# Gating's token mix made in the experts' stage, and one convolution tile on TensorE: a three-stage fp32 kernel

## The chip, the cores and the metric

One core of one Trainium2 chip. The metric is device microseconds of one execution, lower is better. The engines are TensorE (PE; its weight loads PEld), VectorE (DVE), ScalarE (ACT), GpSimd (POOL) and SyncE (SP), which here issues most DMAs. L12 is line 12 of the kernel; a "q" behind an engine is its sequencer.

## The reference

Four residual blocks follow one another on x of 16 sequences (B), 512 steps (T), 512 features (D), in fp32, with `cond` of 16 x 512.

```python
# 1: state space block; the 16 taps of the convolution are the cond rows, per feature
conv = conv_b + sum(x_pad[:, k:k + L, :] * conv_w[k, 0] for k in range(16))
proj = conv @ Wp + bp;  B_t = softplus(proj[..., :64]);  C_t = tanh(proj[..., 64:])
u = x @ Ws + bs
state = decay * state + dt * b_t * u_t          # scan over steps, y = C_t * state
x = x + y @ Wo + bo
# 2: LSTM with 512 units, step by step
x = x + lstm(x, cond, Wx, Wh, b)
# 3: token shift, hashed experts (16, 512 tokens each), gate
xprev = concatenate([cond[:, None, :], x[:, :-1]], axis=1)
xk = x + (xprev - x) * time_maa_k
xr = x + (xprev - x) * time_maa_r
y = scattered_back(square(relu(expert_in @ w_key[e])) @ w_value[e])   # expert_in: rows of xk
x = x + sigmoid(xr @ w_recept.T) * y
# 4: per sequence and feature, over time: softmax of |x|, a chosen place, a mask
x = x + x * (abs(x) >= abs(x) at the place where cumsum(softmax) passes cond)
```

## The kernel before, in words

Features lie on partitions, in KD = 4 blocks of 128. Three stages run one after the other; each is a block of per-engine instruction lists written by hand, with semaphores between the engines, and a stage begins on every engine only when all engines have ended the one before.

**Recurrence** (`recur_phase`). Time is cut into 32 tiles of 16 steps; a tile's 16 steps of all 16 sequences are 256 columns. Block 1 of tile n+2 or n+3 is worked out beside the LSTM steps of tile n. `convolve(m, q, first, last)` is 64 VectorE operations per tile on 128x256 (L595 the first tap, L599 the others), half q = 0, 1 covering two feature blocks. `project(m, q)` (L337) multiplies the result by Wp, `inputs(m, q)` (L345) the window by Ws, `outputs(m, q)` (L357, L358) the state by Wo, `input_products(m, par, q)` (L841 to L843) x1 by Wx, as three products of split halves, q = 0 to 15. ScalarE has `soft_first` (L464 to L468), `soft_last` (L472), `state_high`, `split_high` (L485) and `keep_inputs` (L491, one per input product); VectorE the five parts of `state_part` (from L605), `add_block` (L652), `split_low` (L666) and `split_wx` (L776).

Ahead of the first tile the work of tiles 0, 1 and part of 2 is done in an order of its own. VectorE: convolve(0), two split_wx, state(0), two split_wx, add_block(0), split_low(0), convolve(1), convolve(2, 0), state(1), add_block(1), split_low(1), convolve(2, 1), and then the first step's transpose (L683). TensorE: project(0) and inputs(0) by halves, outputs(0), inputs(1), all 16 input products, project(1), outputs(1), inputs(2), project(2, 0), then the first half of a step (L387). ScalarE issues the loads of Wx and Wh at its beginning. GpSimd waits for Wh and then stores 16 MB of zeros to the experts' rows in memory (L305). SP loads windows (L210) and centers (L203).

The block-2 result x2 goes from `stream` to memory, tile by tile, in 64-byte pieces (L236, the last L248); xk rows go to the experts' buffer by indirect DMA (L298).

**Experts** (`expert_phase`). For each of 16 experts: 512 rows are turned (L926), 8 groups of products with wk, relu and square on ScalarE (L980, L984), 4 groups of products with wv, copied by ScalarE (L994) and stored by GpSimd (L913). Weights are split into halves by ScalarE (L968, L985) and VectorE. SP loads wk (L899) for expert e once wk of e-1 is split, rows (L892), and wv (L904).

**Finish** (`finish_phase`). For each sequence i: SP loads x2; ScalarE scales the shifted x2 (`weigh_last`, L1184), VectorE makes xr from it (`mix_in`, L1250); `receptance(i)` multiplies it by wr on TensorE (L1147, four groups of 128x512 in fp32), two banks in turn, each freed by ScalarE's `open_gate` (L1192). GpSimd gathers the experts' rows (L1107), TensorE turns them (L1158), VectorE's `combine(i)` (L1261, L1264) makes x3. Then block 4: `absolute` (ScalarE, L1199), `invert` (L1268, L1272), `exponent` (L1207), `scan` (L1279), `take_sides` (ScalarE, L1216), `choose`, `search` (L1294), `keep` (L1303), and the product on GpSimd (L1133). The main loop on VectorE is, for each i, scan(i), bound(i), combine(i+1), mix_in(i+3), choose(i), invert(i+1), search(i), keep(i); on ScalarE

```python
            for i in range(B):
                if i + 2 < B:
                    open_gate(i + 2, 0, 2)
                take_sides(i)
                if i + 1 < B:
                    absolute(i + 1)
                if i + 2 < B:
                    open_gate(i + 2, 2, KD)
                if i + 1 < B:
                    exponent(i + 1)
                if i + 4 < B:
                    weigh_last(i + 4)
```

and on TensorE turn(i+2), receptance(i+3).

Of the kernel before, what the change touches and what calls it, by code (L numbers as in the profile page):

```python
# [20 lines left out]
F32 = mybir.dt.float32  # L21
# [54 lines left out]
def build(nc, ins, out):  # L76

    x2_d = nc.dram_tensor("x2_scratch", (P, KD, B, T), F32, kind="Internal").ap()
# [3 lines left out]
    with ExitStack() as ctx:  # L82
# [10 lines left out]
        expert_phase(nc, ctx, ins, carve, banks, keep, rows_d, y_d)  # L93
        carve.top = base
        finish_phase(nc, ctx, ins, carve, banks, keep, x2_d, y_d, out)


def recur_phase(nc, ctx, ins, carve, banks, keep, x2_d, slot_d, rows_d, y_d):
# [5 lines left out]
    wh = carve(KD, 4 * H)  # L104
    wx_lo = carve(KD, 4 * H, dt=F32R)
# [37 lines left out]
    expert_no, slot_base, onehot, segment, count = (carve(E, SEG, at=at + 2048 + 4096 * i) for i in range(5))  # L143

    gate_ps, xw_ps = banks[0:2], banks[2:4]
    proj_ps, u_ps = banks[4][:, 0:LTILE], banks[5][0:N_STATE, 0:LTILE]
# [14 lines left out]
             "rows_turned", "rows_ready", "index_ready", "scattered", "pool_passed", "sp_passed", "center_landed"]  # L161
    s = {n: ctx.enter_context(nc.semaphore("rc_" + n)) for n in names}
    halves = ["window_landed", "x2_stored", "g_done", "turned", "pre_ready", "ifo_ready", "g_ready", "terms_ready",
# [3 lines left out]
    x_dram = ins["xT"]  # L167
# [21 lines left out]

    def two(q):  # L190
        return slice(2 * q, 2 * q + 2)
# [4 lines left out]
    with nc.Block() as block:  # L196
        @block.sync
        def _(sp):
# [6 lines left out]
            def load_window(m, q):  # L205
                sp.wait_ge(s["conv_done"], CONVS * (m - 1) + CONVS // 2 * (q + 1))
                sp.sem_inc(s["sp_passed"], 1)
                sp.wait_ge(s["u_part"], 2 * (m - 1) + q + 1)
# [5 lines left out]
            for q in range(2):  # L214
                sp.dma_start(window[:, two(q), HALO:], x_dram[:, two(q), 0:LTILE]).then_inc(s["window_landed"][q], 16)
            load_center(0)
            for m in range(1, 4):
                for q in range(2):
                    load_window(m, q)
                if m < 3:  # L220
                    load_center(m)
# [10 lines left out]
            def tile(n, pair, four, ahead):  # L232
                if later(n, 1):
                    sp.wait_ge(s["x2_done"], 2 * n)
                    sp.sem_inc(s["sp_passed"], 1)
                    sp.dma_start(x2_d.rearrange("p c b t -> p (c b) t")[:, :, bass.ds((n - 1) * LSTEPS, LSTEPS)],  # L236
                                 stream[four - 1].rearrange("p c b t -> p (c b) t")[:, :, 1:])\
                        .then_inc(s["x2_stored"][(four + 1) % 2], 16)
# [9 lines left out]
            sp.dma_start(x2_d.rearrange("p c b t -> p (c b) t")[:, :, (NLT - 1) * LSTEPS:],  # L248
# [79 lines left out]
        def _(pe):  # L328
# [70 lines left out]
            for q in range(2):  # L399
                project(0, q)  # L400
                inputs(0, q)
# [991 lines left out]
```

## Time and profile before

| | |
|---|---|
| median of 3 runs | 4121.78 us (4120.27 to 4122.02) |
| the profiled execution's own time | 4119.96 us |
| its span, first to last instruction | 4118.3 us |
| mean granted TensorE clock | 0.98 of full speed |
| busy: PE, DVE, ACT, POOL | 94%, 74%, 41%, 7% |
| first step of the recurrence (DVE) | 118.98 us |
| first load of the experts' stage | 3011.67 us |
| first load of the finish | 3783.95 us |
| first and last round's scan in the finish | 3825.25, 4096.19 us |

All stage times are from the profiled execution, counted from its span's start. The profiled execution is 1.8 us shorter than the median of the runs. The three stages do not overlap, so what shortens one shortens the whole.

### The profile page before, as it was taken

To read this page: it belongs to the slowest core of one execution; us is meant where nothing else is said; L and a number is where in the kernel's file an instruction comes from. 1 tells how busy PE (TensorE), PEld (TensorE's weight loads), DVE (VectorE), ACT (ScalarE), POOL (GpSimd) and SP (SyncE) were. 2 spreads that over 40 slices of the span, in tenths; PEclk is the share of its full clock that TensorE was granted. 3 is DMA by queue.
4 is the path that set the end of the run, shared out by engine and by line. 5 is a ranking of instruction groups with operands and counts; after the bars stand their busy time and mean duration, and the time that the engine had idled before them with its cause. 6 is when DMAs were issued, how large, how long until landed. Compare 5 with 4: busy or idle time off the path is not lost. (4 is left out here: it accounts for less than half of the span.)

```text
span 4118.3 us, 111735 instructions
## 1 busy us (share of the span) xinstructions
PE 3858.1 (94%) x44034; PEld 2530.6 (61%) x44034; DVE 3047.6 (74%) x9953; ACT 1677.9 (41%) x5296; POOL 292.5 (7%) x362
## 2 busy tenths in 40 slices
PE   3999999999999999999999999999769999997995
PEld 3566666666656666665666666666457888875442
DVE  9888888888878888887888888875545544552798
ACT  3334433333433333333333333433234434443675
POOL 1000000000000000000000000000000000001343
PEclk8999999999999999999999999999989999998998
DMA  7121111112111111211111112100043343333353
GB/s 287 28 37 27 27 35 27 31 31 37 27 28 27 35 27 32 38 29 28 27 35 27 32 30 37 27 17 15 12 166 123 130 157 141 122 112 123 123 184 112
DMA packets 387862, 266.94 MB, mean 65 GB/s; under 512 B 288953, under 2 KB 322233, under 8 KB 384292
## 3 DMA queue, kind: packets, MB, share of 16 engines
q1 hardware_dynamic: 365648, 184.21, 17.8%
q0 software_dynamic: 17696, 66.79, 4.2%
q10 hardware_dynamic: 4020, 9.10, 0.6%
q8 instruction: 338, 5.54, 0.6%
q14 instruction: 160, 1.31, 0.1%
HBM read 176.48 MB, written 83.92 MB: 63 GB/s over the span
## 5 line engine op out<-in xcount | busy, mean ns | idle before, releaser
L387 PE MATMUL bank<-buf,buf 128*16 128x256 f32 x32768 | 1872.3, 380 | 62.5 <-DVE buf L705 52.9
L387 PEld LDWEIGHTS bank<-buf,buf 128*16 128x16 f32 x32768 | 906.0, 97 | 883.1 <-DVE buf L705 78.9
L841 PE MATMUL bank<-buf,buf 128*128 128x256 f32 (+1 forms) x3072 | 1036.7, 337 | 2.7 <-DVE buf L1012 2.7
L842 PE MATMUL bank<-buf,buf 128*128 128x256 f32 (+1 forms) x3072 | 978.3, 318 | 0.0
L843 PE MATMUL bank<-buf,buf 128*128 128x256 f32 (+1 forms) x3072 | 977.4, 318 | 0.0
L599 DVE SCALAR_TENSOR_TENSOR buf<-buf,buf,buf 128x256 f32<-128x256 f32 x1920 | 870.6, 480 | 0.8 <-issue 0.8
L683 DVE STREAM_TRANSPOSE buf<-bank 128x256 f32<-128x256 f32 x1024 | 459.9, 449 | 449.4 <-PE bank L387 409.3
L556 ACT ACTIVATE buf<-buf 128x96 f32<-128x96 f32 x1024 | 290.4, 284 | 1136.6 <-DVE buf L688 1136.0
L841 PEld LDWEIGHTS bank<-buf,buf 128*128 128x128 f32 x3072 | 581.2, 189 | 253.3 <-issue 215.2
L843 PEld LDWEIGHTS bank<-buf,buf 128*128 128x128 f32 x3072 | 583.3, 190 | 41.3
L842 PEld LDWEIGHTS bank<-buf,buf 128*128 128x128 f32 x3072 | 584.2, 190 | 38.5
L559 ACT ACTIVATE buf<-buf 128x32 f32<-128x32 f32 x1024 | 235.1, 230 | 631.7 <-DVE buf L700 631.7
L1024 DVE CAST buf<-buf 128x512 fp32r<-128x512 f32 x128 | 54.6, 427 | 355.8 <-ACT buf L984 352.3
L688 DVE SCALAR_TENSOR_TENSOR buf<-buf,buf 128x128 f32<-128x128 f32 x1024 | 295.3, 288 | 20.1
L1147 PE MATMUL bank<-buf,buf 128*128 128x512 f32 x512 | 231.6, 607 | 46.6 <-DVE buf L1250 23.8
L298 POOL DMA_INDIRECT expert_in_scratch<-buf,buf x64 | 81.1, 1268 | 2413.1 <-ACT buf L512 2370.2
L491 ACT ACTIVATE buf<-bank,buf 128x256 f32<-128x256 f32 x512 | 234.6, 458 | 19.0 <-PE bank L843 18.6
L705 DVE SCALAR_TENSOR_TENSOR buf<-buf,buf 128x32 f32<-128x32 f32 x1024 | 193.9, 189 | 61.8 <-ACT buf L559 14.2
L700 DVE SCALAR_TENSOR_TENSOR buf<-buf,buf 128x32 f32<-128x32 f32 x1024 | 196.5, 192 | 36.0 <-DVE buf L697 0.7
L557 ACT ACTIVATE buf<-buf 128x32 f32<-128x32 f32 x1024 | 218.3, 213 | 0.0
L1147 PEld LDWEIGHTS bank<-buf,buf 128*128 128x128 f32 x512 | 97.1, 194 | 169.8 <-issue 136.2
L694 DVE SCALAR_TENSOR_TENSOR buf<-buf,buf 128x32 f32<-128x32 f32 x1024 | 176.2, 172 | 18.1 <-ACT buf L556 15.0
(139 smaller groups left out, 2906.5 us busy)
## 6 DMA issues: line engine op xcount, KB each, us to landing
buf<-in_wk SPq DMA_DIRECT2D x16, 2048.0 KB, 9.6
buf<-in_wv SPq DMA_DIRECT2D x16, 2048.0 KB, 9.3
buf<-in_xT SPq DMA_DIRECT2D x62, 496.0 KB, 3.8
buf<-in_xB SPq DMA_DIRECT2D x32, 512.0 KB, 3.6
expert_in_scratch<-buf POOLq DMA_DIRECT2D x16, 1024.0 KB, 22.6
x_scratch<-buf SPq DMA_DIRECT2D x32, 512.0 KB, 9.6
buf<-expert_in_scratch SPq DMA_DIRECT2D x16, 1024.0 KB, 11.6
expert_out_scratch<-buf POOLq DMA_DIRECT2D x64, 256.0 KB, 4.7
```

What stands on the lines that cost most here:

```text
L387: last = mm(gate_ps[hf][32 * j:32 * j + B, 0:HCOLS], hist[:, k, at_step(slot_at)], wh[:, k, j * GCOLS + hf * HCOLS:j * GCOLS + (hf + 1) * ...
L491: a(xw[par][:, :, q, :], xw_ps[q % 2][:, 0:LTILE].rearrange("p (b t) -> p t b", b=B), ACT.Identity, bias=bias[:, q:q + 1], scale=0.5).then ...
L556: a(gate[hf], pre[hf][:, 0:6, :], ACT.Tanh, scale=0.5).then_inc(s["ifo_ready"][hf], 1)
L557: a(gcand[hf], pre[hf][:, 6:8, :], ACT.Tanh).then_inc(s["g_ready"][hf], 1)
L559: a(tanh_c[hf], cell[hf], ACT.Tanh, scale=0.5).then_inc(s["tc_ready"][hf], 1)
L599: v.scalar_tensor_tensor(out=conv[:, k, :], in0=src, scalar=taps[:, k, i:i + 1], in1=conv[:, k, :], op0=ALU.mult, op1=ALU.add).then_inc(s[ ...
L683: v.transpose(turned_g[hf].rearrange("p g b -> p (g b)"), gate_ps[hf][:, 0:HCOLS])\
L688: v.scalar_tensor_tensor(out=pre[hf], in0=turned_g[hf][:, :, 0:B], scalar=0.5, in1=xw[par][:, st, 8 * hf:8 * hf + 8, :], op0=ALU.mult, op1 ...
L841: nc.tensor.matmul(out, left[0], right[0], start=first, stop=False)
L842: nc.tensor.matmul(out, left[0], right[1], start=False, stop=False)
L843: return nc.tensor.matmul(out, left[1], right[0], start=False, stop=last)
L1147: last = nc.tensor.matmul(r_ps[m % 2][:, 0:T], wr[:, k, m * P:(m + 1) * P], xr[i % 2][:, k, :], start=k == 0, stop=k == KD - 1)
```

## The change

Four things are done.

1. In the start, convolve(1) leaves VectorE. ScalarE scales the identity by each of the 64 taps (`diag`, in the room that Wh takes later), TensorE makes the convolution of tile 1 with them (`convolve1`), from a window of its own, and ScalarE copies it out with the bias. Wh's load moves behind those copies. The order of products, gates and copies ahead of the first tile changes.
2. x2's rows in memory get one column more, at the front, that holds the halo (the first store writes it).
3. In the experts' stage xr is made for one sequence per expert: SP loads x2 of sequence e, ScalarE scales (`weigh_last`), VectorE mixes (`mix_in`), SP stores it to `xr_scratch`.
4. A class `Gating` holds wr, xr, stream and gate in room that the last expert has left; its first loads and receptance(0) and (1) with their gates run at the end of the experts' stage. The finish loads xr and has neither `weigh_last` nor `mix_in` nor halos.

```diff
-    x2_d = nc.dram_tensor("x2_scratch", (P, KD, B, T), F32, kind="Internal").ap()
+    x2_d = nc.dram_tensor("x2_scratch", (P, KD, B, 1 + T), F32, kind="Internal").ap()
+    xr_d = nc.dram_tensor("xr_scratch", (P, KD, B, T), F32, kind="Internal").ap()
...
+            def convolve1(k):
+                pe.wait_ge(s["window1_landed"][k // 2], 16)
+                for i in range(TAPS):
+                    pe.wait_ge(s["diag_ready"], TAPS * k + i + 1)
+                    last = mm(conv_ps[k], diag[:, TAPS * k + i, :], window1[:, k, i * B:i * B + LTILE],
+                              start=i == 0, stop=i == TAPS - 1)
+                last.then_inc(s["conv1_summed"], 1)
...
-            for q in range(2):
-                project(0, q)
-                inputs(0, q)
+            convolve1(0)
+            project(0, 0)
+            inputs(0, 0)
+            convolve1(1)
+            convolve1(2)
+            project(0, 1)
+            inputs(0, 1)
+            convolve1(3)
             pe.wait_ge(s["steps"], 7)
             for q in range(2):
                 outputs(0, q)
             for q in range(2):
                 inputs(1, q)
+            for q in range(2):
+                project(1, q)
             pe.wait_ge(s["wx_ready"], KD)
-            for q in range(NBLK):
+            pe.wait_ge(s["conv1_ready"], KD)
+            for q in range(NBLK // 2):
                 input_products(0, 0, q)
             for q in range(2):
-                project(1, q)
-            for q in range(2):
                 outputs(1, q)
+            for q in range(NBLK // 2, NBLK):
+                input_products(0, 0, q)
...
-            act.dma_start(wh, ins["Wh"]).then_inc(s["wh_landed"], 16)
...
+            for k in range(KD):
+                for i in range(TAPS):
+                    a(diag[:, TAPS * k + i, :], ident, ACT.Copy, scale=taps[:, k, i:i + 1]).then_inc(s["diag_ready"], 1)
...
             state_high(0)
+            act.wait_ge(s["proj_part"], 2)
+            for k in range(KD):
+                act.wait_ge(s["conv1_summed"], k // 2 * 2 + 2)
+                a(conv[:, k, :], conv_ps[k], ACT.Identity, bias=conv_b[:, k:k + 1]).then_inc(s["conv1_ready"], 1)
+            act.dma_start(wh, ins["Wh"]).then_inc(s["wh_landed"], 16)
             for q in range(2):
                 split_high(0, 0, q)
-            for q in range(NBLK):
-                keep_inputs(0, 0, q)
             soft_first(1)
             soft_last(1)
+            for q in range(NBLK // 2 - 2):
+                keep_inputs(0, 0, q)
             state_high(1)
+            for q in range(NBLK // 2 - 2, NBLK):
+                keep_inputs(0, 0, q)
             for q in range(2):
                 split_high(1, 1, q)
...
-            for q in range(2):
-                convolve(1, q, 0, CONVS // 2)
             convolve(2, 0, 0, CONVS // 2)
...
+                if later(e, 1):
+                    sp.wait_ge(s["xr_made"], KD * e)
+                    store_mixed(e - 1)
+                else:
+                    sp.dma_start(maa_r, ins["maa_r"]).then_inc(s["maa_landed"], 16)
+                load_x2(e)
 
             experts(sp, one)
+            sp.wait_ge(s["turned"], KD * E)
+            sp.wait_ge(s["wk_ready"], KD * E)
+            sp.wait_ge(s["xr_stored"], 16 * (E - 1))
+            sp.dma_start(gating.wr, ins["wr"]).then_inc(gating.s["wr_landed"], 16)
+            for i in range(gating.XR_RING):
+                gating.load_mixed(sp, xr_d, i)
+            sp.wait_ge(s["h_summed"], KF * E)
+            for i in range(2):
+                gating.load(sp, x2_d, i)
+            sp.wait_ge(s["xr_made"], KD * E)
+            store_mixed(E - 1)
+            sp.wait_ge(s["xr_stored"], 16 * E)
...
             experts(pe, one)
+            pe.wait_ge(s["xT_ready"], KD * E)
+            pe.wait_ge(gating.s["wr_landed"], 16)
+            for i in range(2):
+                gating.receptance(pe, i)
...
             experts(act, one)
+            for i in range(2):
+                gating.open_gate(act, i, 0, KD)
...
+            def mix_in(e, k):
+                dve.wait_ge(s["weighed"], KD * e + k + 1)
+                v.scalar_tensor_tensor(out=xr_row[:, k, :], in0=x2_row[:, k, 1:], scalar=maa_now[:, k:k + 1],
+                                       in1=xr_row[:, k, :], op0=ALU.mult, op1=ALU.add).then_inc(s["xr_made"], 1)
...
             for i in range(B):
-                sp.wait_ge(s["final_ready"], i + 1)
+                sp.wait_ge(final_ready, i + 1)
                 sp.dma_start(out.rearrange("p (k b t) -> p k b t", k=KD, b=B)[:, :, i, :], final).then_inc(stored, 16)
                 if i + RING < B:
-                    load(i + RING)
+                    gating.load(sp, x2_d, i + RING)
+                    gating.load_mixed(sp, xr_d, i + RING)
...
-            receptance(0)
             turn(0)
-            receptance(1)
             turn(1)
-            receptance(2)
+            gating.receptance(pe, 2)
...
-                if i + 4 < B:
-                    weigh_last(i + 4)
...
-                if i + 3 < B:
-                    mix_in(i + 3)
```

In an expert, `weigh_last(e, a)` follows the copy of y(e, a) on ScalarE, and the four `mix_in(e, k)` follow the split of the next wk on VectorE. `Gating.load_mixed(i)` waits, for i of 3 and more, until receptance(i - 3) is summed.

## Rows read from the trace of the kernel before

**Rows 1.** Windows: us, length, then busy (count) of PE, PEld, DVE, ACT, POOL, clock, DMA share, GB/s
```profile
3124.00:3171.00 47.00, 45.72 (x210) 37.49 (x210) 23.48 (x36) 20.14 (x32) 2.17 (x4) 1.00 0.36 133
3860.00:4000.00 140.00, 128.22 (x391) 62.61 (x390) 138.35 (x259) 103.97 (x262) 68.16 (x49) 1.00 0.51 181
```

**Rows 2.** Timeline of VectorE, start: start us, length us, engine, line, operation, count
```profile
60.33 0.73 DVE L595 TENSOR_SCALAR buf<-buf,buf,buf 128x256 f32<-128x256 f32 x2
...
86.02 0.73 DVE L595 TENSOR_SCALAR buf<-buf,buf,buf 128x256 f32<-128x256 f32 x2 [0.56 <-PE bank L337]
...
98.55 0.41 DVE L605 TENSOR_TENSOR buf<-buf,buf 64x256 f32<-64x256 f32 x1
...
118.98 0.45 DVE L683 STREAM_TRANSPOSE buf<-bank 128x256 f32<-128x256 f32 x1
```

**Rows 3.** Timeline of VectorE in the finish; in brackets idle time and what ended it
```profile
3858.13 4.54 DVE L1279 TENSOR_TENSOR_SCAN buf<-buf,bank 128x512 f32<-128x512 f32 x4
...
4065.33 4.55 DVE L1279 TENSOR_TENSOR_SCAN buf<-buf,bank 128x512 f32<-128x512 f32 x4
...
4076.20 0.17 DVE L1268 TENSOR_SCALAR buf<-buf 128x4 f32<-128x4 f32 x1 [0.71 <-ACT buf L1199]
...
4080.76 4.55 DVE L1279 TENSOR_TENSOR_SCAN buf<-buf,bank 128x512 f32<-128x512 f32 x4
```

**Rows 4.** Timeline of TensorE in one round, then groups of ScalarE (mean ns)
```profile
3942.06 7.03 PE L1147 MATMUL bank<-buf,buf 128*128 128x512 f32 x16
3950.61 7.13 PE L1147 MATMUL bank<-buf,buf 128*128 128x512 f32 x16 [1.51 <-ACT buf L1192]
3957.58 1.91 PE L1158 MATMUL bank<-buf,buf 128*128 128x128 f32 x16
...
L1216 ACT ACTIVATE buf<-buf,buf 128x512 f32<-128x512 f32 x64 | 45.3, 712 | 3.2 <-DVE buf L1284 3.2
...
L1199 ACT ACTIVATE buf<-buf 128x512 f32<-128x512 f32 x64 | 39.4, 620 | 1.7 <-DVE buf L1264 1.1 <-issue 0.6
```

**Rows 5.** Timeline of ScalarE, start and end of the recurrence
```profile
22.79 7.31 ACT L537 ACTIVATE buf<-buf 128x2048 fp32r<-128x2048 f32 x4 [6.42 <-DMA buf<-in_Wx]
...
80.76 0.48 ACT L491 ACTIVATE buf<-bank,buf 128x256 f32<-128x256 f32 x1 [0.96 <-PE bank L843]
...
2990.55 1.30 ACT L503 ACTIVATE buf<-buf,buf 128x128 f32<-128x128 f32 x4
```

**Rows 6.** Timeline of TensorE, start
```profile
31.57 2.05 PE L337 MATMUL bank<-buf,buf 128*128 128x256 f32 x4 [21.35 <-DVE buf L599]
...
84.88 1.89 PE L337 MATMUL bank<-buf,buf 128*128 128x256 f32 x8
...
104.27 3.54 PE L345 MATMUL bank<-buf,buf 128*64 128x256 f32 x8
```

**Rows 7.** Edge of experts and finish: a drain, TensorE's start, three windows, gathers to landing
```profile
L885 POOLq DRAIN  x1: 5279/5279/5279, 3778.4 to 3778.4; - x1
...
3798.74 2.05 PE L1147 MATMUL bank<-buf,buf 128*128 128x512 f32 x2 [23.77 <-DVE buf L1250]
...
3799.00:3804.00 5.00, 5.00 (x7) 1.90 (x7) 1.20 (x2) 1.96 (x4) 0.00 (x0) 0.50 1.04 385
3804.00:3807.00 3.00, 3.00 (x8) 1.42 (x7) 1.53 (x3) 1.20 (x2) 0.00 (x0) 0.97 0.84 260
...
3824.00:3829.00 5.00, 0.06 (x2) 0.04 (x1) 4.01 (x7) 3.72 (x10) 0.00 (x0) 0.91 0.30 112
...
buf<-expert_out_scratch,buf POOLq DMA_INDIRECT x8, 7.5
```

**Rows 8.** DMA issues at the end of the recurrence: the last store of x2, us to landing
```profile
x_scratch<-buf SPq DMA_DIRECT2D x1, 512.0 KB, 7.8
```

**Rows 9.** Experts: SP's load of wk(2), ScalarE's split of it
```profile
3061.64 0.39 SPq L899 DMA_DIRECT2D buf<-in_wk  x1
...
3101.24 3.89 ACT L968 ACTIVATE buf<-buf 128x1024 fp32r<-128x1024 f32 x4
```

More of the change, by code:

```diff
@@ L104, in recur_phase @@
     wh = carve(KD, 4 * H)
+    diag = carve(TAPS * KD, P, at=carve.last)
     wx_lo = carve(KD, 4 * H, dt=F32R)
@@ L344, in inputs @@
                 for k in (2 * q, 2 * q + 1):
-                    last = mm(u_ps, ws[:, k, :], window[:, k, HALO:], start=k == 0, stop=k == KD - 1)
+                    last = mm(u_ps, ws[:, k, :], (window1 if second else window)[:, k, HALO:], start=k == 0,
+                              stop=k == KD - 1)
                 last.then_inc(s["u_part"], 1)
+            def convolve1(k):
[5 more added lines that the diff above has]
+                last.then_inc(s["conv1_summed"], 1)
             def outputs(m, q):
@@ L968, in split_wk, with weigh_last @@
                     nc.scalar.activation(wk_hi[:, k, :], wk_raw[:, k, :], ACT.Copy).then_inc(s["wk_hi_ready"], 1)
+            def weigh_last(e, k):
+                if k == 0:
+                    if not later(e, 1):
+                        act.wait_ge(s["share_ready"], 2)
+                    act.wait_ge(s["x2_landed"], 16 * (e + 1))
+                    if later(e, 1):
+                        act.wait_ge(s["xr_stored"], 16 * e)
+                nc.scalar.activation(xr_row[:, k, :], x2_row[:, k, 0:T], ACT.Copy, scale=maa_last[:, k:k + 1])\
+                    .then_inc(s["weighed"], 1)
             split_wk(0)
@@ L1034, in one, with finish_phase @@
                     split_wk(e + 1)
+                for k in range(KD):
+                    mix_in(e, k)
             experts(dve, one)
-def finish_phase(nc, ctx, ins, carve, banks, keep, x2_d, y_d, out):
+def finish_phase(nc, ctx, ins, carve, banks, keep, gating, x2_d, xr_d, y_d, out):
     ident, cond, place = keep["ident"], keep["cond"], keep["place"]
-    RING, NC = 6, T // P
-    wr = carve(KD, D)
-    maa_r, maa_last, maa_now = carve(KD), carve(KD), carve(KD)
-    stream = [carve(KD, 1 + T) for _ in range(RING)]
-    weighed = carve(KD, T)
-    xr = [carve(KD, T) for _ in range(2)]
-    gate = [carve(KD, T) for _ in range(2)]
+    RING, NC = gating.RING, T // P
+    stream, gate, landed = gating.stream, gating.gate, gating.landed
     rows = [[carve(D) for _ in range(NC)] for _ in range(2)]
```

231 lines of the change are left out of this document (124 added, 107 removed).

## The prediction

> **What bounds the kernel now.** I read first the page's busy rows and slices, then a table of windows by stage, then the timelines of the edges between stages, and the chain of waits last (it shows only the finish). Three stages follow one another: recurrence (119 to 3008 us), experts (3012 to 3776 us), finish (3784 us to the end).
>
> The start up to 119 us is VectorE's: it runs 32 convolution operations at a time, and the first step of the recurrence (its first transpose, at 118.98) comes right behind the last of them [rows 2]. TensorE mostly waits, at 1.2 GHz.
>
> The experts are TensorE's: 45.7 of 47 us busy, at 2.4 GHz, with VectorE and ScalarE at half or less [rows 1]. The change adds no product there.
>
> The finish has a repeating round, seen in the scans: 3858.13 to 4065.33 is 12 rounds, 17.27 us each. In a round VectorE is never idle, TensorE idles once (1.5 us, for ScalarE's gate) and works the rest [rows 3, 4]. So VectorE sets the pace and TensorE is right behind it. Rounds 13 and 14, which have no token mix left, take 15.43 us [rows 3]; they have no receptance products either, so they alone do not tell the new pace.
>
> **Start: what the convolution's move does.** VectorE loses convolve(1): 60.33 to 86.02, 25.7 us [rows 2]. What takes its place has to be followed through ScalarE and TensorE. I call *d* the delay of the first tile's soft plus.
>
> 1. ScalarE makes 64 scaled diagonals of 128x128 from 16.4 us on. The nearest row is four scaled 128x128 copies in 1.30 us [rows 5]: with one's length of 0.40 that is 0.30 apart, so 19.2 us, to 35.6. Then the four halves of Wx (7.3 us [rows 5]), to 42.9; the soft plus wanted ScalarE at 46.1. Hidden. At 0.40 each the diagonals end at 42, Wx at 49.3, the table load at 50.6: d = 4.5. Nothing lies below 0.
>
> 2. TensorE: a 128x256 product in full precision shows as two instructions; 8 of them take 1.89 us at 2.4 GHz, 4 take 2.05 us at 1.2 GHz [rows 6]. So 0.43 us a matmul, 6.9 us for a feature block's 16 taps, 27.5 us for all four, and twice that at 1.2 GHz. Block 0 starts at 18.8; from idle the clock needs some 5 us to come back (3798.74 to about 3804 [rows 7]), so it ends near 28.5. The first half of project(0) waits for VectorE till 31.5; then comes 1.7 us of work and blocks 1 and 2 (13.8 us), to 47.0 instead of 44.0, where project(0)'s second half stood. The soft plus begins at 47.9 instead of 46.1: d = 1.8. The pause from 28.5 to 31.5 is 3 us; the clock fell about 4.5 us into the idle time after 3824 [rows 7], so I take it as held. If it fell, d = 4.3.
>
> The Trainium skill, TensorE: Matmul & The Clock Gate, Part 1, says that the reduced clock is the default and only activity lifts it. The trace agrees (0.50 in 3799 to 3804, 0.97 in the next three). By that rule read strictly, the sparse products before 45 us leave it low, and all of the convolution costs double; that is the second rival.
>
> 3. Block 3 (6.9 us) then lies beside the state's 7.3 us chain (46.1 to 53.4), and conv1's four copies behind it; Wh's load, moved behind them (to about 57 us), lands by 70, long before the recurrence. The zero stores queued behind it on GpSimd (22.6 us median landing) end near 110 and are wanted first by add_block(2), at step 11 of the first tile. The zeros' share of the queue falls on window loads that are wanted ten us later. Priced at nothing; if a window is late, +2.
>
> 4. VectorE now: split_low(0) ends at 60.3 + d; convolve(2,0) 12.5 us, 72.9 + d; state(1) to the end of outputs(1), 98.55 to 104.27 = 5.7 us [rows 2, 6], less 1 at full clock: 77.7 + d. Here something new waits: split_low(1) needs ScalarE's split_high(1), and that is now queued behind all 16 keep_inputs, so behind input products 8 to 15. They are 1.44 us apart [rows 5]: 11.5 us, 89.2 + d; the copy 0.5, split_high 2 x 0.6, split_low 0.7: 91.6 + d; convolve(2,1) 12.5: 104.1 + d. VectorE idles 12 us of the 25.7 saved. With d = 1.8 the recurrence begins at 105.9 instead of 119.0 (-13.1); with d = 4.5 and products 8 to 15 starting at 1.2 GHz (+2.3) at 110.9 (-8.1). I take **-11.5**, nearer the held clock.
>
> **Recurrence and its end.** Steps are unchanged. x2's rows become 513 elements, so its 64-byte pieces lie off their old alignment. The last store lands 7.8 us after 2991.95, [rows 8], before the last scatter's (issued 3001.85), and the next stage begins at 3011.67. It may take more than twice as long for nothing; but it can slow the last scatters (2.7 to 5.4 us each). 0 to +4, I take **+0.5**. A page's rule speaks against it: the Trainium skill, DMA: Bandwidth & Descriptors, How a descriptor splits into AXI transactions, says that one not starting on a 256-byte boundary is fetched from the boundary below, with unused bytes. No row here shows such a start. By it a 2,048-byte row of x2 costs up to one transaction in nine more, in loads that nothing waits for.
>
> **Experts.** Added per expert: four scaled 128x512 ScalarE copies (0.7 us), four VectorE mixes (0.68), 2 MB. ScalarE has 4.8 us between two y copies, VectorE more. On SP's queue store_mixed(e-1) waits for the end of expert e-1, and behind it are x2(e), wk(e+1) and its rows. wk(2) was issued at 3061.64 and is now at about 3077.7; 4 MB at the 390 GB/s of [rows 7] is 10.8 us plus 2, so 3090.5, and it is wanted at 3101.24 [rows 9]: 10.7 us of room. Nothing. maa_r lands with wv(0), for which ScalarE waits anyway.
>
> **The edge to the finish.** TensorE ended y at 3775.0 and stood still until 3798.74 [rows 4, 7]; now receptance(0) and (1) follow at once: 64 instructions of 0.43 us, 27.5 us, to 3802.5, ScalarE's last gate 3803.1. The stage cannot end before that; GpSimd's drain (5.3 us from 3778.4 [rows 7]) is hidden in it. So the new stage begins at 3803.4, 19.5 us later than 3783.9. From there: gathers(0) issued by +4.7, landed 7.5 later [rows 7] (+12.3), first turn 0.9 (1.2 GHz), combine(0): 3816.7. From combine(0) to scan(0) it was 9.3 us, of which mix_in(2) showed 1.6: now 7.7. Scan(0) at 3824.4 where it was 3825.25: 1 us gained. But receptance(1), whose second half held the next round (10 us from 3828.96, at a low clock), is done. TensorE: turn(1) until 3822.4, receptance(2) 13.8 + 1 for the clock: ends P = 3837.2.
>
> **The new round.** With P the end of a receptance: turn 1.75, first two groups 6.87, second two at once since the gate no longer stands behind weigh_last: 15.6 us with the 0.1 seen between receptance and turn [rows 4]. On ScalarE: second gate ends P + 9.2, four sides at 0.70, four absolutes at 0.61 [rows 4]: P + 14.5; from there to the scan VectorE needs 4.6 (4076.17 to 4080.76 [rows 3]): P + 19.1 = P' + 3.5. VectorE alone would need 15.43. So **TensorE sets 15.6**, and half of mix_in's 2.73 comes back. Bounds: 15.43; above, 16.2 if the third MB per round (269 GB/s with the output, where 181 was 0.51 of the queues [rows 1], so 0.76) stretches gathers.
>
> Scan(1) is P + 3.6 = 3840.8 instead of 3858.13: -17.3. Scan(1) to scan(14): 13 x 15.6 = 202.8 instead of 222.6: -19.8. The last round and the 22.1 us behind scan(15) stay. Finish: **-37.1** (bounds: scan(1) -2 to +3, pace -2 to +8: -41 to -26).
>
> **Sum.** -11.5 + 0.5 - 37.1 = -48.1 against the profiled execution's own 4119.96: 4071.9. The median of the runs is 1.8 above it: **4073.7 us**. 0.2% (8 us) is what a measurement here tells from no change.
>
> **Rivals.**
> - *The round stays near 17.* Gathers or the extra load, or ScalarE's order, hold it at 17.0 to 17.3. For: TensorE and VectorE are both near full, with loops between three engines. Against: the one wait TensorE has goes away by name. 13 x 17.27 = 224.5: finish -15.4, sum -26: about 4095. Chance 0.08.
> - *The convolution runs at 1.2 GHz.* Blocks 1 and 2 take 27.5 us: project(0) ends its wait at 63, d = 18, recurrence at 122 or later: +3 instead of -11.5: 4088. For: all of TensorE's short bursts before 45 us run at that clock [rows 6]. Against: TensorE would be busy without a break there, and elsewhere it rises after 5 us. Chance 0.10.
> - *More than I count*, by pace 15.43, warm products, or an earlier edge: 4060 to 4066. Chance 0.10.
> - *Slower than before.* The wk load, moved behind the mixed store, comes too late: TensorE stalls in each expert. It decides from 48/14 = 3.4 us a stall, so a landing 14 us later than 3090.5; then 4122 and up. For: the queue is in order. Against: 4 MB would have to take 27 us. Chance 0.02.
>
> My own case 0.70, with a range of its own of 4065 to 4086 (start -8.1 to -13.1, finish -32 to -41, the stores +4). The range 4063 to 4089 takes in most of the clock rival. Faster 0.97, same 0.015, slower 0.015.
>
> **What would show it.** First transpose of the recurrence near 107 us, VectorE idle before split_low(1) for 10 us or more. TensorE in the experts unchanged (about 47 us each). The first gather about 29 us after the last y copy instead of 9. Scans 15.6 us apart, TensorE without idle, VectorE waiting for ScalarE's absolutes. Scan(1) only 16.5 us behind scan(0), where it was 32.9. Wrong would be: convolution products of twice 0.215 us after 36 us; a wait on a weight load in the experts; turns waiting for gathers.

## The result: 42% slower, and the profile after

The changed kernel takes 5837.2 us (median of 4 runs, 5820.2 to 5852.2) where the kernel before takes 4121.0 beside it: ratio 1.4164, 95% interval 1.4139 to 1.4188. Forecast were 4073.7 us and faster. The page of the changed kernel, in the same slices as before: the two rows at the end are DMA queues, with packets, MB and share of 16 engines' span (for q1 it was 17.8% before).

```profile
span 5846.5 us, 112046 instructions
PE 4112.0 (70%) x44162; PEld 2631.7 (45%) x44162; DVE 3026.9 (52%) x9889; ACT 1712.1 (29%) x5364; POOL 292.4 (5%) x346
...
PE   7845645777766677684554577766677639999987
...
DMA  6699799677899667769978967999875795555475
...
q1 hardware_dynamic: 390992, 234.61, 76.8%
...
q8 instruction: 339, 5.55, 0.8%
```

The loss is all in the recurrence, where TensorE's digits are 4 to 8 and the DMA row's 5 to 9. The windows of one tile of the recurrence show how it comes about (columns as in [rows 1]); the first fence is the timeline of SP's queue with x2's stores, L252 and L255 (in the kernel before L236):

```profile
322.18 0.54 SPq L255 DMA_DIRECT2D x_scratch<-buf  x1
...
501.98 0.54 SPq L255 DMA_DIRECT2D x_scratch<-buf  x1
```
```profile
300.00:320.00 20.00, 19.98 (x276) 12.78 (x280) 15.73 (x62) 7.89 (x31) 1.00 (x1) 1.00 0.12 41
320.00:340.00 20.00, 16.98 (x212) 10.02 (x204) 11.55 (x40) 3.80 (x17) 0.41 (x2) 1.00 1.78 35
340.00:360.00 20.00, 2.12 (x33) 1.03 (x34) 3.69 (x15) 2.92 (x9) 0.00 (x0) 0.68 2.20 5
360.00:380.00 20.00, 0.00 (x0) 0.00 (x0) 0.00 (x0) 0.00 (x0) 0.00 (x0) 0.50 2.23 5
380.00:400.00 20.00, 1.61 (x16) 0.71 (x19) 0.00 (x0) 0.00 (x0) 0.00 (x0) 0.50 2.33 6
400.00:420.00 20.00, 13.17 (x115) 7.13 (x108) 6.78 (x29) 5.83 (x16) 0.00 (x0) 0.84 0.88 3
```

This tile lasts 180 us, from store to store, where one lasted 90; the mean over all tiles is 146. Its one store, 512 KB in 8,192 pieces of 64 bytes, is issued at 322.18, and from then to about 410 the DMA engines are full (a share above 1 means that packets of one engine overlap in the records) and move 3 to 6 GB/s from 340 on. The last such store of before landed after 7.8 us [rows 8]. Some 20 us into the store the four compute engines fall silent, for all of 360 to 380, and TensorE's granted clock falls to 0.50 (1.2 GHz). The waits of the changed kernel from 100 to 4600 us say on what (us in all, times, the longest one):

```profile
ACT buf L612 <- DVE buf L745: 2066.8, 494, 80.7
DVE buf L740 <- PE bank L423: 1757.9, 429, 81.8
PEld bank L423 <- issue: 1303.1, 826, 80.0
PE bank L423 <- issue: 999.3, 121, 79.5
```

ScalarE waits for VectorE, VectorE for TensorE, and TensorE for "issue": no semaphore, nothing that the profile shows. One such wait, in TensorE's timeline:

```profile
398.39 3.59 PE L423 MATMUL bank<-buf,buf 128*16 128x256 f32 x31 [54.66 <-issue]
```

Over the four lines of products (L423 and L896 to L898) such waits come to 1,416 us on the page, where the kernel before has 9. The products of the steps also take longer, 2,065 us (L423) instead of 1,872, at a lower mean clock (0.86 instead of 0.98). The two together are 1,600 of the some 1,766 us that the recurrence lost, from its first step to the first load of the experts' stage (106.60 to 4765.2 us, before 118.98 to 3011.67).

The DMA queues say what is missing: those of the changed kernel in 360 to 400, and below them those of the kernel before in 300 to 340, which holds a whole store of x2.

```profile
q1 hardware_dynamic: 3075, 0.20, 226.0%
q8 instruction: 1, 0.02, 1.7%
```
```profile
q1 hardware_dynamic: 8442, 0.96, 23.1%
q8 instruction: 4, 0.07, 0.8%
q14 instruction: 2, 0.02, 0.2%
```

A queue's share times 16 x 40 us, over its packets: the one instruction packet of this window took 10.9 us instead of 1.3, a packet of q1 0.47 us instead of 0.018. (Over the whole execution the mean of an instruction packet is 2.2 us instead of 1.2.) What counts more is that they stay away. From 321 to 373 us the changed kernel has no instruction packet at all, first fence; the kernel before has nine in the same stretch, second fence:

```profile
q1 hardware_dynamic: 5811, 0.86, 210.2%
```
```profile
q8 instruction: 6, 0.10, 0.8%
q14 instruction: 3, 0.02, 0.2%
```

The next one lasts from 374 to 385, and TensorE goes on at 398. It is the same in all 42 of TensorE's "issue" waits of more than 10 us in the recurrence: by the packets' times, an instruction packet ends within the wait, and TensorE goes on 1 to 16 us after the last one that has ended. The Trainium skill, Runtime: NRT & Kernel Launch, Instruction fetch mechanics, says that each engine's sequencer fetches its instructions in blocks of 16 KiB over a DMA queue of its own. The rows agree (one packet of 0.02 MB). So the reading is that new instructions come through the DMA engines, and that TensorE runs dry while its block waits behind x2's pieces. This last link rests on the order in time: the records don't say which engine a packet is for, and no run held back the instructions alone.

The start and the finish came out as forecast. VectorE's split_low(1) and the first transpose, then the finish's second scan and the next, and a window of its rounds, against [rows 2], [rows 3] and [rows 1]:

```profile
92.87 1.29 DVE L723 TENSOR_TENSOR buf<-buf,buf 128x512 fp32r<-128x512 f32 x2 [11.66 <-ACT buf L529]
...
106.60 0.45 DVE L740 STREAM_TRANSPOSE buf<-bank 128x256 f32<-128x256 f32 x1
```
```profile
5589.48 4.55 DVE L1374 TENSOR_TENSOR_SCAN buf<-buf,bank 128x512 f32<-128x512 f32 x4 [0.95 <-ACT bank L1317]
5606.82 4.55 DVE L1374 TENSOR_TENSOR_SCAN buf<-buf,bank 128x512 f32<-128x512 f32 x4
5622.32 4.55 DVE L1374 TENSOR_TENSOR_SCAN buf<-buf,bank 128x512 f32<-128x512 f32 x4
```
```profile
5640.00:5780.00 140.00, 140.00 (x435) 70.40 (x434) 131.46 (x254) 95.39 (x253) 76.10 (x46) 1.00 0.78 256
```

TensorE is busy for all of 140 us where it was for 128.2, a round takes 15.50 us instead of 17.27, and scan(1) comes 17.3 us behind scan(0) instead of 32.9.

### The profile page after: what moved, and what is told of

Read it like the earlier page. It is cut to its first block and busy times, and to the rows that moved or that the text cites. A ratio compares the mean times of both kernels' runs of the same rounds, so it can differ in the third digit from the quotient of the medians.

```text
span 5846.5 us, 112046 instructions
## 1 busy us (share of the span) xinstructions
PE 4112.0 (70%) x44162; PEld 2631.7 (45%) x44162; DVE 3026.9 (52%) x9889; ACT 1712.1 (29%) x5364; POOL 292.4 (5%) x346
## 5 line engine op out<-in xcount | busy, mean ns | idle before, releaser
L423 PE MATMUL bank<-buf,buf 128*16 128x256 f32 x32768 | 2064.9, 396 | 1152.7 <-issue 1024.8
L423 PEld LDWEIGHTS bank<-buf,buf 128*16 128x16 f32 x32768 | 953.1, 99 | 2149.8 <-issue 1338.0
L896 PE MATMUL bank<-buf,buf 128*128 128x256 f32 (+1 forms) x3072 | 1053.7, 343 | 133.8 <-issue 128.1
L897 PE MATMUL bank<-buf,buf 128*128 128x256 f32 (+1 forms) x3072 | 994.1, 324 | 138.3 <-issue 138.2
L898 PE MATMUL bank<-buf,buf 128*128 128x256 f32 (+1 forms) x3072 | 994.3, 324 | 125.0 <-issue 125.0
L656 DVE SCALAR_TENSOR_TENSOR buf<-buf,buf,buf 128x256 f32<-128x256 f32 x1860 | 846.8, 481 | 0.8 <-issue 0.8
L896 PEld LDWEIGHTS bank<-buf,buf 128*128 128x128 f32 x3072 | 594.7, 194 | 278.8 <-issue 236.4
L898 PEld LDWEIGHTS bank<-buf,buf 128*128 128x128 f32 x3072 | 597.1, 194 | 265.7 <-issue 221.7
L897 PEld LDWEIGHTS bank<-buf,buf 128*128 128x128 f32 x3072 | 598.0, 195 | 166.5 <-issue 125.3
L762 DVE SCALAR_TENSOR_TENSOR buf<-buf,buf 128x32 f32<-128x32 f32 x1024 | 194.1, 190 | 62.8 <-ACT buf L615 13.1
L757 DVE SCALAR_TENSOR_TENSOR buf<-buf,buf 128x32 f32<-128x32 f32 x1024 | 196.5, 192 | 36.0 <-DVE buf L754 0.7
L754 DVE SCALAR_TENSOR_TENSOR buf<-buf,buf 128x32 f32<-128x32 f32 x1024 | 189.3, 185 | 0.0
L751 DVE SCALAR_TENSOR_TENSOR buf<-buf,buf 128x32 f32<-128x32 f32 x1024 | 176.1, 172 | 4.4 <-ACT buf L612 1.3
L1169 DVE SCALAR_TENSOR_TENSOR buf<-buf,buf,buf 128x512 f32<-128x512 f32 x64 | 48.0, 750 | 205.3 <-ACT buf L1116 205.3
## 6 DMA issues: line engine op xcount, KB each, us to landing
buf<-expert_in_scratch SPq DMA_DIRECT2D x16, 1024.0 KB, 14.7
```

What stands on the lines that cost most here:

```text
L423: last = mm(gate_ps[hf][32 * j:32 * j + B, 0:HCOLS], hist[:, k, at_step(slot_at)], wh[:, k, j * GCOLS + hf * HCOLS:j * GCOLS + (hf + 1) * ...
L656: v.scalar_tensor_tensor(out=conv[:, k, :], in0=src, scalar=taps[:, k, i:i + 1], in1=conv[:, k, :], op0=ALU.mult, op1=ALU.add).then_inc(s[ ...
L896: nc.tensor.matmul(out, left[0], right[0], start=first, stop=False)
L897: nc.tensor.matmul(out, left[0], right[1], start=False, stop=False)
L898: return nc.tensor.matmul(out, left[1], right[0], start=False, stop=last)
```

## The experiments

**1. Is it the layout of x2?** The change gives x2's rows in DRAM a column in front (513 elements, the data from element 1), so that an expert's load brings the time step before the first with it. One kernel puts only this into the kernel before; one takes only this out of the changed kernel; two keep the kernel before and place the data on or off multiples of 64 bytes.

```
-    x2_d = nc.dram_tensor("x2_scratch", (P, KD, B, T), ...)
+    x2_d = nc.dram_tensor("x2_scratch", (P, KD, B, 1 + T), ...)   # e3, e4, e10: 16 + T
     stores and loads of row i: x2_d[..., i, OFF:OFF + T]          # e1: 1, e3: 16, e4: 8, e10: 4
```

> The kernel before with x2's rows in memory one element longer (513) and the data from element 1 on, nothing else changed (no halo stored). Theory A (the 64-byte pieces of x2's stores, no longer on 64-byte boundaries, are written some ten times slower, and while they are under way the engines' instructions arrive late): the whole loss without the gains, 5837 + 48 = about 5885 us, DMA share near 2 for some 100 us after each store. Rival B (the loss comes from the new start, the experts' new loads or the wider use of memory): 4121 us.

> The changed kernel with x2's rows in memory as before (512 elements, pieces on 64-byte boundaries); the halo is not stored but written by ScalarE into column 0 of the experts' row, one small operation per expert. Theory A: the forecast of the change without this cost, 4070 to 4080 us (start -12, finish -37). Rival B (another part of the change is slow): well above 4121, up to 5837 us.

> The kernel before with rows of 528 elements (2112 bytes, a multiple of 64) and the data from element 16 on: every piece starts on a 64-byte boundary, but rows are no longer 2048 bytes apart. Theory A (alignment): 4121 us. Rival C (the distance between rows, off a power of two or off 256 bytes): about 5885 us.

> Rows of 528 elements, data from element 8 on: pieces start 32 bytes off a 64-byte boundary. Theory A with a unit of 64 bytes: as slow as the changed layout, about 5885 us. Theory A with a unit of 32 bytes or less (only the 4-byte offset costs): 4121 us.

Measured: the layout alone 5875.1 us, ratio 1.426 (1.418 to 1.434). The change without the column, with ScalarE writing the first element of the row from the condition instead, 4079.6 us, 0.990 (0.989 to 0.992). Rows of 528 elements with the data 64 bytes in 4121.3, and 32 bytes in 4123.5, both the same as before. So the column explains the whole loss, everything else in the change is a gain of 1%, and longer rows or a start 32 bytes off cost nothing.

**2. Does the store's queue matter?** The store in the bad layout, issued by ScalarE instead of SP, so that the window loads don't stand behind it.

> The misaligned layout alone (513 elements a row), but x2's stores issued from ScalarE's queue instead of SyncE's, where window and center loads no longer stand behind them. Rival D (the loads of windows and centers queue behind the slow store in SyncE's queue, and the steps wait for them): back near 4140 us. Theory A (the slow store keeps the DMA engines busy, and instructions arrive late, whichever queue it is on): within 5% of 5875 us.

5870.9 us, 1.425 (1.416 to 1.433): no difference, so order on SP's queue is not the cause. The waits of that kernel are again those of the changed one:

```profile
PE bank L381 <- issue: 1043.4, 121, 82.4
```

**3. What of the layout costs?** At first I held that each piece that starts off a grid has a fixed price and that the stage lasts as long as its stores.

> The kernel before with x2's rows in DRAM of 544 elements and its store and its loads cut in two halves by feature blocks: blocks 0 and 1 start at element 16 of a row, so their 64-byte pieces lie on multiples of 64 bytes, blocks 2 and 3 start at element 17, so theirs lie 4 bytes off. The output is unchanged. Theory A (each piece that starts off the grid costs extra time of the DMA engines, about 0.18 us of an engine a piece, and the stage lasts as long as its stores): half as many such pieces, 256 KB a tile; a store of them takes some 50 us of the 94 us that a tile has, so the DMA engines have enough room to finish, and the loss is half or less of that of the layout alone, 4121 to 5000 us, nearer to the lower end if the wait for instructions is what makes the loss, since the engines are then free in half of the time. Rival B (any store off the grid spoils the whole stage, however much it carries): about 5875 us.

> The kernel before with x2's rows of 528 elements and the data from element 4, so that every 64-byte piece starts 16 bytes behind a multiple of 32 and of 64. The output is unchanged. If the grid that counts is 32 bytes, about 5875 us as with the 4-byte offset; if it is 16 bytes or finer, 4121 us. The 32-byte offset cost nothing and so can't tell the two apart.

> The e8 kernel with the rows of the mixed r input in DRAM of 513 elements and the data behind the first: the store of a row (1 MB, in pieces of 2048 bytes) now starts off every multiple of 32 bytes in nearly all rows, as its loads do. The output is unchanged. Theory A (a fixed price for each piece's edges, so that it counts in small pieces alone): 2048-byte pieces are 32 times fewer for their bytes, the store and the loads stay hidden in an expert's 188 us, 4073 us. Rival (a price by the byte, 5 GB/s as the 64-byte stores showed): 1 MB takes 200 us of all DMA engines a time, and the time rises by hundreds of us or more.

Half of the pieces 4 bytes off: 4130.5 us, ratio 1.003. All pieces 16 bytes off: 4301.2 us, 1.044, neither of the two values named. Pieces of 2048 bytes off, in rows 2052 bytes apart: 4071.9 against 4073.0 without (experiment 4), nothing in the time. The transfers do suffer. One window of four experts (188 us; one takes 47), without and with the offset, has the DMA share go from 0.50 to 0.70 at the same GB/s:

```profile
3200.00:3388.00 188.00, 182.88 (x835) 150.10 (x834) 105.60 (x160) 91.35 (x149) 8.67 (x16) 1.00 0.50 178
```
```profile
3200.00:3388.00 188.00, 182.89 (x835) 150.00 (x834) 105.58 (x160) 91.20 (x148) 8.67 (x16) 1.00 0.70 179
```

The median landing of the xr stores goes from 5.6 to 15.8 us. Over the 8,192 pieces of these stores the page's q1 share gives 0.30 us more a piece (the loads are in it too), no less than what a 64-byte piece pays in rows 2052 bytes apart (0.22, in the table below). So the price goes by the piece rather than by the byte. What saves the large pieces here is their number, 512 in a store instead of 8,192, and the room beside it. For small pieces, a constant offset costs far less than rows of 513 elements. Two things are in that layout: starts that are no multiple of 16 bytes, and rows 2052 bytes apart, so that the start moves from row to row. Four kernels took them apart (OFF and the row's length changed in the diff above; in e15 both halves of e9 start at element 17).

> The kernel before with x2's rows of 528 elements and the data from element 1, so that every 64-byte piece starts exactly 4 bytes behind a multiple of 64, in every row. The output is unchanged. In the layout of the change the rows have 513 elements, so the start moves by 4 bytes from row to row, and one piece in 16 lies on a multiple of 64. Theory A1 (what costs is a start off a fine grid, 4 bytes as in 15 or fewer of 16 pieces there): as slow as that layout or slower, 5850 to 6000 us. Theory A2 (what costs is the odd length of the row, which lays rows 2052 bytes apart, and the start itself only what the 16-byte offset cost): about 4300 us.

> The same with the data from element 2, every piece 8 bytes behind a multiple of 64. The output is unchanged. If the price depends on the grid on which the start lies: between the 16-byte offset (4301 us) and the 4-byte one, which tells how the price falls with the grid; if 16 bytes is the last grid that the write path knows, the same as the 4-byte offset.

> The kernel with half of the pieces off (4130 us), with the other half put 4 bytes off as well: two stores of 256 KB a tile, rows of 544 elements, all pieces 4 bytes behind a multiple of 64. The output is unchanged. If the price is by the piece and straight, twice the loss of the half, 4140 us, and then the layout of the change is slow by its odd rows; if the loss runs away once a store outlasts what hides it, some thousand us more, as with one store of 512 KB.

> The kernel before with x2's rows of 516 elements and the data from element 0: rows 2064 bytes apart, so a quarter of the rows each lie 0, 16, 32 and 48 bytes behind a multiple of 64. The output is unchanged. If only the start counts, half of the pieces lie 16 bytes off a grid of 32 and the loss is half of that of the constant 16-byte offset or less, 4121 to 4210 us; if uneven row distances make the loss, well over 4300 us.

4, 8 and 16 bytes off cost the same (4313.0, 4309.1, 4301.2 us). The grid is 32 bytes, and how far off a piece starts doesn't matter. Rows of 516 elements, half of whose pieces are off, cost 7 us; two stores of 256 KB, all off, 139 us. That left the distance of the rows:

```
e17:  x2_d = dram_tensor("x2_scratch", (P * KD * B * T + 16,)).ap()[1:1 + P * KD * B * T]   # rows of 512
e18:  x2_d = dram_tensor("x2_scratch", (P, KD, B, 17 + T)), OFF = 1                         # rows of 529
```

> The kernel before with its x2 scratch shifted as a whole: rows of 512 elements as before, the first at element 1 of the buffer, so every 64-byte piece starts 4 bytes behind a multiple of 64 and rows stay 2048 bytes apart. The output is unchanged. Theory C (off-grid pieces meet in the same part of the memory when rows lie about 2048 bytes apart, which rows of 513 elements keep nearly and rows of 528 do not): several hundred to 1750 us over the kernel before. Theory A2 (rows an odd distance apart make the loss): 4313 us, as with rows of 528.

> The kernel before with x2's rows of 529 elements and the data from element 1: rows 2116 bytes apart, so the start moves by 4 bytes from row to row as with rows of 513 elements, but the distance is far from 2048. The output is unchanged. Theory A2 (a distance that is no multiple of 16 bytes): about 5875 us, as with rows of 513. Theory C (distances near 2048 bytes): about 4300 us.

4417.7 us, 1.072 (1.069 to 1.076), and 4234.0 us, 1.028 (1.022 to 1.034). All of these, in order of the price of a piece, which is worked out from the page's q1 share: (share x span x 16 engines, less the same of the kernel before) over the 262,144 pieces of 32 stores (for e9 and e16 over the half that is off). It is the time of a packet; where packets of one engine overlap, the engine itself is held for less. Landing is the page's median for a store, where it has one; the next column is how long the pieces of one store last, from the first packet to the last, in the quickest and the slowest tile.

| rows apart, bytes | pieces start off 32 bytes | landing, us | packets of a store last, us | price, us of an engine | time, us |
|---|---|---|---|---|---|
| 2048 (before) | none | 9.6 | 6 to 8 | 0 | 4121 |
| 2112 (e4), 32 off | none | 10.8 | 6 to 9 | 0.005 | 4123 |
| 2064 (e16) | half, 16 off | 13.9 | 10 to 12 | 0.033 | 4127 |
| 2176 (e9), two stores | half, 4 off | - | 8 to 15 | 0.033 | 4130 |
| 2116 (e18) | 7 of 8, varying | 21.0 | 16 to 20 | 0.039 | 4234 |
| 2176 (e15), two stores | all, 4 off | - | 12 to 26 | 0.049 | 4259 |
| 2112 (e10, e14, e13) | all, 16, 8, 4 off | 23.3, 23.0, 23.2 | 18 to 22 | 0.049 | 4301, 4309, 4313 |
| 2048 (e17) | all, 4 off | 23.3 | 17 to 37 | 0.069 | 4418 |
| 2052 (e1) | 7 of 8, varying | - | 43 to 112 | 0.221 | 5875 |

Two things are read from it. First, the price of a piece is not fixed: it goes from 0.03 to 0.22 us with the distance of the rows. An odd distance alone (2116) is the cheapest of those with nearly all pieces off, a distance of 2048 alone costs 1.4 times that of 2112; 2052 has both and costs three times more again. Neither of the theories that e17 and e18 were to decide between holds by itself: odd distances should have given some 5875 us in e18, distances near 2048 bytes at least several hundred us in e17 (297 came), and at 2064 bytes (e16) the price is low.

The price also moves with the place in the row, within one run. A tile's pieces lie 64 bytes behind those of the tile before. In the changed kernel the stores come 203 and 170 us apart here, and 204 and 169 us apart again sixteen tiles, or 1,024 bytes, later, where most other tiles take 123 to 153:

```profile
699.59 0.58 SPq L255 DMA_DIRECT2D x_scratch<-buf  x1
902.48 0.59 SPq L255 DMA_DIRECT2D x_scratch<-buf  x1
1072.23 0.57 SPq L255 DMA_DIRECT2D x_scratch<-buf  x1
...
3028.41 0.57 SPq L255 DMA_DIRECT2D x_scratch<-buf  x1
3232.32 0.57 SPq L255 DMA_DIRECT2D x_scratch<-buf  x1
3401.65 0.57 SPq L255 DMA_DIRECT2D x_scratch<-buf  x1
```

In e17 and e15 short and long stores take turns: 17 to 20 and 27 to 37 us in e17, 12 to 14 and 23 to 26 us in e15. So the cause has to do with the addresses of the pieces of one store taken together. Which property of them it is, no run shows.

Second, the time doesn't follow the DMA engines' work: with stores of up to 15 us at most 11 us are lost in all, and from 16 us on (e18) TensorE pauses in most tiles. e15 has both in one run: behind its short stores TensorE has hardly a pause, behind the long ones 3 to 10 us. The windows with a store in them, of e16 and then of e17, and the wait in e17's window from 318 to 340:

```profile
300.00:310.00 10.00, 9.68 (x144) 5.89 (x147) 7.80 (x31) 2.80 (x12) 0.00 (x0) 1.00 1.64 86
310.00:320.00 10.00, 10.00 (x152) 6.30 (x147) 7.78 (x32) 6.32 (x20) 0.00 (x0) 1.00 0.02 2
```
```profile
310.00:320.00 10.00, 9.69 (x135) 5.71 (x133) 7.68 (x31) 2.92 (x12) 0.00 (x0) 1.00 1.97 61
320.00:330.00 10.00, 5.04 (x63) 2.99 (x62) 4.47 (x17) 3.33 (x11) 0.00 (x0) 1.00 2.12 22
330.00:340.00 10.00, 2.97 (x28) 1.14 (x29) 0.74 (x2) 0.21 (x2) 0.00 (x0) 0.55 0.81 10
```
```profile
PE bank L388 <- issue: 10.8, 2, 10.2
```

In e17 (store issued at 308.86) TensorE works on for 18 us after the issue, more than 10 us of them beside full DMA engines, and then stops, as it would if it had instructions in hand and got no new ones. A store that is over by then costs nothing, one that lasts longer costs the rest: e9's 256 KB that are off fit into that room, e15's 512 KB don't in every second tile.

The Trainium skill, Collectives: The Full Stack, Rules for kernel authors, wants the buffers of a collective aligned to 32 bytes, which prevents a read-modify-write. It isn't said of a kernel's own stores, but the grid is the one found here: 32 bytes off 4123 us, 16 bytes off 4301.

**4. What is the rest of the change worth?** With the column gone, its two halves alone, and then the small new buffers of the experts' stage (x2_row, xr_row, maa_*) carved behind all others instead of ahead of them.

```
-    x2_row, xr_row = carve(KD, 1 + T), carve(KD, T)
-    maa_r, maa_last, maa_now = carve(KD), carve(KD), carve(KD)
     relu = [carve(CAP) ...
     ...
     y = [carve(D) for _ in range(2)]
+    x2_row, xr_row = carve(KD, 1 + T), carve(KD, T)
+    maa_r, maa_last, maa_now = carve(KD), carve(KD), carve(KD)
```

> The kernel before with only the start of the change (tile 1's convolution on TensorE with diagonals, the new order ahead of the first tile); x2's layout, the experts and the finish as before. My working: 9 to 12 us less, 4109 to 4112 us. Rival (TensorE's clock low through the convolution): 4120 to 4124 us.

> The kernel before with only the token mix in the experts' stage and the gating's first products there, x2's layout as before (halo by ScalarE). My working of the finish alone: 37 us less, 4084 us; with the 0.14 us that each of 64 y groups took longer in the run without the column (9 us in all): 4093 us.

> The run without the column, with the new small buffers of the experts' stage (x2's and xr's row, the shares) carved behind all others, so that the hidden halves lie at the same offset modulo 512 as before. If their place in SBUF makes each y group 5.58 instead of 5.44 us: back to 5.44, some 9 us less, 4071 us. If it is ScalarE's or VectorE's or the DMAs' new work beside them: unchanged, 4080 us.

The start alone 4110.1 us, 0.997 (0.996 to 0.998); gating alone 4092.4, 0.993 (0.991 to 0.995); all with the small buffers last 4073.0 us, 0.988 (0.987 to 0.990). The last differs from e2 in addresses alone and is 6.5 us faster (8 by the ratios). ScalarE's copies of y, one per group of TensorE's products, show where: first e2, then e8.

```profile
3761.20 0.60 ACT L1141 ACTIVATE buf<-bank 128x512 f32<-128x512 f32 x1 [4.11 <-PE bank L893]
3766.78 0.60 ACT L1141 ACTIVATE buf<-bank 128x512 f32<-128x512 f32 x1 [4.38 <-PE bank L893]
```
```profile
3754.60 0.60 ACT L1141 ACTIVATE buf<-bank 128x512 f32<-128x512 f32 x1 [3.98 <-PE bank L893]
3760.04 0.60 ACT L1141 ACTIVATE buf<-bank 128x512 f32<-128x512 f32 x1 [4.23 <-PE bank L893]
```

A group takes 5.58 us in e2 and 5.44 in e8, as before: 0.14 x 64 groups = 9 us. Carved ahead, the new buffers move the hidden layer's halves, which these products read, by 16,512 bytes, 128 more than a multiple of 512; the other buffers carved behind them move as well. What in these addresses matters, no run shows.

**5. A better order at the edge.** TensorE ran both first receptances (27.6 us) before the finish could start.

```
-            for i in range(2):
-                gating.receptance(pe, i)
+            gating.receptance(pe, 0)
     ... finish, TensorE:
+            gating.receptance(pe, 1)
             turn(0)
             turn(1)
```

> The e8 kernel (the change without the column in x2's rows, small buffers placed last) with the second receptance tile and its gate moved from between the experts and the finish to the start of the finish, ahead of the first turns on TensorE and on ScalarE. A receptance tile of 64 matmuls takes 13.8 us of TensorE, during which VectorE has nothing to do; now the first scan's inputs are there 13.8 us earlier, and the tile fills TensorE's time behind it. Expected: the first scan starts some 13 us earlier, the second scan comes later behind it by as much or not at all; if TensorE is what sets the pace of the finish (rounds of 15.5 us with TensorE busy), the work is only moved and the time stays at 4073 us within 2; if the edge was idle time of TensorE, about 4061 us.

4058.4 us, 0.985 (0.983 to 0.987), 14.7 us faster than e8. VectorE's scans, of e8 and then of e11:

```profile
3814.20 4.55 DVE L1372 TENSOR_TENSOR_SCAN buf<-buf,bank 128x512 f32<-128x512 f32 x4 [0.95 <-ACT bank L1315]
3831.91 4.55 DVE L1372 TENSOR_TENSOR_SCAN buf<-buf,bank 128x512 f32<-128x512 f32 x4
```
```profile
3801.85 4.55 DVE L1372 TENSOR_TENSOR_SCAN buf<-buf,bank 128x512 f32<-128x512 f32 x4 [0.95 <-issue]
3817.35 4.55 DVE L1372 TENSOR_TENSOR_SCAN buf<-buf,bank 128x512 f32<-128x512 f32 x4
```

The second receptance now fills the time in which TensorE waited for the first gathers (12.5 us in e8), and the first rounds are already 15.50 us apart. This is the fastest kernel of the study, 1.5% ahead of the one before.

## Why the prediction was wrong

**The step that failed** is "Recurrence and its end: x2's rows become 513 elements, so its 64-byte pieces lie off their old alignment ... 0 to +4, I take +0.5". The layout alone costs 1754 us. Its bounds went wrong in two ways. The price of the store was bounded by a row of aligned stores ("it may take more than twice as long for nothing"): the row of 7.8 us says nothing of how a store off the grid goes, and such stores took 43 to 112 us. And only the last store was asked about: the other 31 lie in the recurrence, one in each tile of 90 us, and TensorE stops some 15 to 20 us after a store has filled the DMA engines. The rule that I weighed, on starts off a 256-byte boundary, speaks of what is fetched. The loads of 2048 bytes bear out that this is small (those of xr landed in 8.2 us in e12 instead of 7.2, at no cost in time), and I took the store to go like them. The trace held a warning of size: 262,144 pieces of 64 bytes, two thirds of all packets of the program, are changed by this one edit. No rival had this place; the one that ended slower was the wk load, which came in time. Above all the range and the chance of 0.015 for slower were built from the terms that had been worked out, none of which had measured a store off its grid.

**The other steps**, read in e2 and e8, which lack only the column, and in the changed kernel itself:
- *Start, -11.5 (-8.1 to -13.1)*: the first transpose comes at 106.60 in the changed kernel (-12.4; forecast near 107), at 109.69 in e8 (-9.3) and at 110.85 in e5 (-8.1). VectorE waits 11.7 to 13.6 us for split_high(1), as described. The forecast took the clock as held over TensorE's pause of 3 us at 28.5. In the changed kernel it was (granted 1.00 from 32 to 36 us), in e8 it fell (0.61), and that is the "if it fell" of the prediction. Alone the start gave 12.0 us by the ratio. The rival of a convolution at 1.2 GHz throughout did not come true.
- *Experts, nothing*: TensorE's share is the same with the buffers last, 45.73 of 47 us against 45.72 [rows 1]; ahead of the others they cost 9 us that I did not see. Nothing waits for wk. (The load was reckoned at 390 GB/s; [rows 7] have 385, which makes 0.1 us.)
- *Edge and rounds, -37.1 (-41 to -26, though the range of the forecast took -32 as its end)*: scan(1) 26.2 us earlier than before in e8, of which the start gave 9.3: -16.9 (forecast -17.3). From there 13 rounds take 201.7 us (4033.64 less 3831.91; forecast 202.8). TensorE sets the pace, without idle time, as said. The rival of rounds near 17 did not come true.
- *Sum*: without the column and the shifted addresses, 4073.0 us was measured where the sum said 4073.7. So close is in part luck: in e8 the start gained 2 us less than forecast and the rounds 1 us more, and with the addresses as the change has them (e2) it is 4079.6. The right terms were the small ones.

## What to carry over

Before a layout in DRAM is changed, count the pieces that are written to it and where each starts: many small pieces belong on multiples of 32 bytes, and one extra element per row is better written by an engine (e2) than stored with the row. A transfer that nobody waits for can still stop the engines: compare how long it fills the DMA queues with how long TensorE goes on alone, here some 15 us. And a piece of work ahead of a stage's first wait belongs behind it (e11).

## What the hardware showed that I had not expected

- Stores of 64-byte pieces: 4, 8 and 16 bytes off a 32-byte grid cost the same, 0.049 us of a DMA engine a piece with rows 2112 bytes apart; 0.069 at 2048, 0.221 at 2052, 0.039 at 2116. What makes 2052 three to six times dearer stays open.
- Pieces of 2048 bytes off the grid, in rows 2052 bytes apart, pay about as much each (0.30 us, e12); it hid behind the experts.
- The price changes with the place in the row and repeats after 1,024 bytes (rows 2052 bytes apart), or in every second tile of 64 bytes (2048).
- Beside full DMA engines the instruction packets stay away (none in 52 us, where there were nine) and TensorE's "issue" waits rise from 9 us to 1,416.
- The same products take 5.58 or 5.44 us a group with nothing but buffer addresses changed (e2, e8).
